# Splitting the attention row maxima on GpSimd with two maxima buffers, in a three-layer attention and expert kernel

## The chip, the cores and the metric

The kernel runs on one core of a Trainium2 chip. The metric is the device time of one execution in microseconds. A core has TensorE (PE in the profile, with PEld for its weight loads), VectorE (DVE), ScalarE (ACT), GpSimd (POOL) and SyncE (SP), which here only issues DMAs. Each engine works through its own instruction list in order, and they meet at semaphores.

## The reference, cut to what matters

The input x has 8 sequences of 512 rows of 256 numbers. Four layers follow one another; the change touches the softmax of the first, second and fourth.

```python
# layer 1: causal attention, 16 heads of 16
attn = jnp.einsum('bhqd,bhkd->bhqk', q, k) * scale
attn = jnp.where(causal, attn, -jnp.inf)
a = jnp.clip(attn, -100.0, 100.0)
m = jnp.max(a, axis=-1, keepdims=True)
e = jnp.exp(a - m)
p = e / (jnp.sum(e, axis=-1, keepdims=True) + 1e-06)
p = p + 1e-08
attn = p / jnp.sum(p, axis=-1, keepdims=True)
# layers 2 and 4: attention without a mask, then router and experts
probs = jax.nn.softmax(scores, axis=-1)
# layer 3: attention over the 8 sequences with relative positions
```

## The kernel before, in words

The function `attention` runs twice: once for layers 1 and 2 together (16 items, n = 0 to 15, one sequence of one layer each; items 0 to 7 are causal; names end in `_af`), and once for layer 4 (8 items, n = 16 to 23; names end in `_f`). Between and behind them stand the experts and layer 3, which the change leaves alone.

An item has 4 groups g of 4 heads, and a group has 4 slots kt, so 16 slots an item. All engines walk over the slots in an order written out by hand. The scores are needed twice. First as queries by keys, to get the row maximum: TensorE writes them to one of three PSUM banks `sc` (`score`, L474, with the mask at L477), and VectorE takes the negated maximum (`row_max`, L769). Slots of group g make the maxima of the group two further on, so the maxima of group g + 2 are complete when slot 3 of group g ends. Then as keys by queries, straight into the exponential: TensorE writes `sct` (`score_t`, L495), ScalarE takes the exponential (L690), VectorE clips it against a floor in causal items (`clip`, L798), and TensorE multiplies by the values (`pv`, L526). The negated maximum enters the second product as three extra rows of the stationary operand. These rows must be bf16, so the float maximum is split into three bf16 parts.

`split_max` (L771 to L786, VectorE) does this once a group, after the last `row_max` of kt = 3: a clip to plus or minus 100 in causal items (L775), a cast (L780), a subtraction (L782), a cast (L784), a subtraction (L786), each on 128x16 numbers and each waiting for the one before. One slot later TensorE transposes the parts (`use_bank` "max", L438, after `score_t` and `score` of head 0), ScalarE copies them (L655) and SP loads them into `stack_q` (L292).

GpSimd has its own list (L1176 to L1198), once an item n: `inv_std_y`, `lay_out_v`, `split` (three operations that split q or k in three parts, L1050 to L1054), `add_floor` (L1101 and L1106, causal), `inv_std_x`, `add_bias`, `scale_y`, `sum_v`, `scatter`. Three of its orders are waited for elsewhere:

- `add_floor(n - 1, 3)` completes the output of item n - 1. TensorE transposes that output at the head of slot 4 of item n (L457), waiting for `att_added` (L455).
- `inv_std_y(n - 2)` gives `shift1`, for which ScalarE waits in `norm_y` (L609, run at L616) in slots 1 and 2 of item n, in items whose predecessor but one has experts.
- ScalarE reads q or k of j = 2 and 3 from PSUM into `qkf`, which has two buffers, and waits until `split` of j - 2 has read the buffer (L664). In the opening of `attention` ScalarE reads j = 3 of item first + 1 before its first exponential (L727 to L745).

Of the kernel before, what the change touches and what calls it, by code (L numbers as in the profile page):

```python
# [49 lines left out]
def attention(nc, M, R, S, C, A, layers, first, end, units):  # L50
# [175 lines left out]
    with nc.Block(no_gpsimd_drain=True) as block:  # L226
# [533 lines left out]
        def _(dve):  # L760
            def row_max(n, g, qt, i):
                heads = score_heads(n, qt, i)
                if not heads:
                    return
                u = max_unit(n, g, qt, i)
                dve.wait_ge(S.sc_ps, u + 1)
                cols = P * (qt + 1) if causal(n) else T
                src = M.sc[u % 3][:, 0:len(heads) * cols].rearrange("p (h k) -> p h k", h=len(heads))
                nc.vector.tensor_reduce(M.neg_max[:, qt, heads[0]:heads[-1] + 1], src, AX.X, ALU.max, negate=True).then_inc(S.max_done, 1)  # L769

            def split_max(n, g):  # L771

                dve.wait_ge(S.max_done, max_unit(n, g, 3, 3) + 1)
                if causal(n):
                    nc.vector.tensor_scalar(M.neg_max[:, :, :], M.neg_max[:, :, :], -100.0, 100.0, ALU.max, ALU.min).then_inc(S.max_clip, 1)  # L775
                    dve.wait_ge(S.max_clip, NG * n + g + 1)
                if NG * n + g > 0:
                    dve.wait_ge(S.max_ps, NG * n + g)
                st = 4 * (NG * n + g)
                nc.vector.tensor_copy(M.max_parts[:, :, 0, :], M.neg_max[:, :, :]).then_inc(S.max_split, 1)  # L780
                dve.wait_ge(S.max_split, st + 1)
                nc.vector.tensor_tensor(M.max_rest[:, :, :], M.neg_max[:, :, :], M.max_parts[:, :, 0, :], ALU.subtract).then_inc(S.max_split, 1)  # L782
                dve.wait_ge(S.max_split, st + 2)
                nc.vector.tensor_copy(M.max_parts[:, :, 1, :], M.max_rest[:, :, :]).then_inc(S.max_split, 1)  # L784
                dve.wait_ge(S.max_split, st + 3)
                nc.vector.tensor_tensor(M.max_parts[:, :, 2, :], M.max_rest[:, :, :], M.max_parts[:, :, 1, :], ALU.subtract).then_inc(S.max_split, 1)  # L786

            def clip(n, g, kt, half):

# [156 lines left out]
            def slot(n, g, kt):  # L946
                s = KT * g + kt
                tn, tg = group(n, g + 2)
                pn, pg = group(n, g - 1)
                if kt > 0 and causal(n):  # L950
                    clip(n, g, kt - 1, 1)
                for i in range(4):
                    if exists(tn):
                        row_max(tn, tg, kt, i)
                    if i == 1:
                        if s - y_slot(n) in (2, 4):
                            add_y(n - 1, (s - y_slot(n) - 2) // 2)
                        if s == 9:
                            sum_key(n - 2)
                        if s == 10:  # L960
                            choose(n - 2)
                        if s == 14 and n == last:
                            place_early()
                        if 2 <= s < 6:
                            x_stats(n + 2, (s - 2,))
                    if i == 2:
                        if causal(n):
                            clip(n, g, kt, 0)
                        if kt == 2:
                            normalise(pn, pg)  # L970
                        if 4 <= s - y_slot(n) < 8:
                            y_stats(n - 1, (s - y_slot(n) - 4,))
                if kt == KT - 1 and exists(tn):
                    split_max(tn, tg)

            def split_first(j):

# [19 lines left out]
            for g in (0, 1):  # L997
                for qt in range(KT):
                    for i in range(4):
                        row_max(first, g, qt, i)  # L1000
                split_max(first, g)
            for n in range(first, end):
                if n == 1:
                    dve.wait_ge(S.consts_loaded, C.loads)
# [13 lines left out]
        def _(pool):  # L1018
# [24 lines left out]
            def split(n, j):  # L1043
                if not exists(n):
                    return
                st = 3 * (splits(n, j) - 1)
                pool.wait_ge(S.qkf_ready, 4 * n + j + 1)
                full, top = M.qkf[:, j % 2, :], M.parts[:, j, 0, :]

                nc.gpsimd.tensor_tensor(M.parts[:, j, 1, :], full, top, ALU.subtract).then_inc(S.split_step, 1)  # L1050
                pool.wait_ge(S.split_step, st + 1)
                nc.gpsimd.tensor_tensor(full, full, top, ALU.subtract).then_inc(S.split_step, 1)
                pool.wait_ge(S.split_step, st + 2)
                nc.gpsimd.tensor_tensor(M.parts[:, j, 2, :], full, M.parts[:, j, 1, :], ALU.subtract).then_inc(S.split_step, 1)  # L1054

            def lay_out_v(n, g):
                if not exists(n):
# [114 lines left out]
            for g in range(NG - 1):  # L1172
                lay_out_v(first, g)
            sum_v(first)
            split(first + 1, 0)
            for n in range(first, end):  # L1176
                if n == 1:
                    pool.wait_ge(S.consts_loaded, C.loads)
                inv_std_y(n - 2)
                lay_out_v(n, 3)  # L1180
                split(n + 1, 1)
                split(n + 1, 2)
                add_floor(n - 1, 3)
                split(n + 1, 3)
                inv_std_x(n + 2)
                add_floor(n, 0)
                add_bias(n - 1)
                scale_y(n - 2)
                lay_out_v(n + 1, 0)
                lay_out_v(n + 1, 1)  # L1190
                add_floor(n, 1)
                sum_v(n + 1)
                lay_out_v(n + 1, 2)
                add_floor(n, 2)
                if n == last:
                    inv_std_y(last - 1)
                scatter(n - 2)
                split(n + 2, 0)  # L1198
            add_bias(last)
            scale_y(last - 1)  # L1200
# [9 lines left out]
def attention_memory(nc, ctx, R, tag, dram):  # L1210

    def sb(name, shape, dt=F32):
        return ctx.enter_context(nc.sbuf_tensor(f"{name}_{tag}", shape, dt))

    def psum(name):
        return ctx.enter_context(nc.psum_tensor(f"{name}_{tag}", [P, T], F32))

    gen = [psum("gen0"), psum("gen1")]
    M = Names()
    M.q_parts_d, M.k_parts_d, M.src_d = dram  # L1220

    M.x_in = R.w1[NW - 1][:, 0, :].rearrange("p (t d) -> p t d", t=KT)
    M.xn = R.w1[NW - 1][:, 1, :].rearrange("p (t d) -> p t d", t=KT)
    M.res = sb("res", [P, KT, D])
    M.st0 = sb("st0", [P, KT, 6])
    M.mv0 = sb("mv0", [P, KT, 2])
    M.var0 = sb("var0", [P, KT])
    M.rstd0 = sb("rstd0", [P, KT])
    M.mean0, M.shift0 = sb("mean0", [P, KT]), sb("shift0", [P, KT])
    M.xnT = sb("xnT", [P, DC, T])  # L1230
    M.qkf = sb("qkf", [P, 2, T])
    M.parts = sb("parts", [P, 4, 3, T], BF16)
    M.v_st = sb("v_st", [P, KT, D])
    M.v_aug = sb("v_aug", [P, KT, H, 32])

    shared = R.w2[:, :, :, :].rearrange("p c e d -> p (c e d)")
    o1, o2 = 2 * 4 * T, 2 * 4 * T + (KT - 2) * H * 32
    M.floor = shared[:, 0:o1].rearrange("p (g h t) -> p g h t", g=2, h=4)
    M.v_later = shared[:, o1:o2].rearrange("p (t h e) -> p t h e", t=KT - 2, h=H)
    M.v_pair = shared[:, o2:o2 + 2 * D].rearrange("p (a d) -> p a d", a=2)  # L1240
    M.v_tot = shared[:, o2 + 2 * D:o2 + 3 * D]
    M.v_all = shared[:, o2 + 3 * D:o2 + 5 * D].rearrange("p (a d) -> p a d", a=2)

    M.stack_q = sb("stack_q", [99, NG, 4, T], BF16)
    M.stack_k = sb("stack_k", [99, NG, 4, T], BF16)

    M.neg_max = sb("neg_max", [P, KT, 4])
    M.max_rest = sb("max_rest", [P, KT, 4])
    M.max_parts = sb("max_parts", [P, KT, 3, 4], BF16)
    M.max_sb = sb("max_sb", [12, 2, T], BF16)  # L1250
    M.prob = sb("prob", [P, 2, 4, T])
    M.o_sb = sb("o_sb", [P, T])
    M.floor_w = sb("floor_w", [P, KT, 4])
    M.e8 = sb("e8", [P, KT, 4])
    M.den = sb("den", [P, KT, 4])
    M.rden = sb("rden", [P, KT, 4])
    M.floor_v = sb("floor_v", [P, KT, 4, HD])
    M.att = [sb(f"att{i}", [P, KT, D]) for i in range(2)]
    M.attT = sb("attT", [P, DC, T])

    M.sc = [psum("sc0"), psum("sc1"), psum("sc2")]
    M.sct = [psum("sct0"), psum("sct1")]
    M.out = psum("out")
    M.gen = gen
    M.gen_bf = [t[:, :].bitcast(BF16) for t in gen]
    return M
# [1327 lines left out]
```

## Time and profile before

| what | us |
|---|---|
| median of 3 runs (2644.34 to 2658.11) | 2650.02 |
| the profiled execution, its own time | 2654.06 |
| its span in the profile | 2652.3 |
| TensorE busy | 2465.1 (93% of the span) |
| VectorE busy | 1835.1 (69%) |
| ScalarE busy | 1438.0 (54%) |
| GpSimd busy | 1332.1 (50%) |

The two runs of `attention` fill about 40 to 1150 us and 1825 to 2370 us of the span. The profile gives each group of instructions with its line, engine and count, the waits by releaser, and a timeline of each engine. The mean granted TensorE clock was 0.971 of full speed, where 1.00 stands for 2.4 GHz and 0.50 for 1.2 GHz.

### The profile page before, as it was taken

Reading aid. Unit: us, or ns where it says so; the run is one execution under the profiler, and the core shown is the slowest. Engines: PE = TensorE matmul, PEld = TensorE weight load, DVE = VectorE, ACT = ScalarE, POOL = GpSimd, SP = SyncE. Lnnn points to the kernel's source line nnn. Section 1 sums busy time; section 2 is a strip of 40 time slices with the busy share of each in tenths; the row PEclk is TensorE's granted clock in tenths of the full one; section 3 lists DMA queues with packets and bytes.
Section 4 is the critical chain, followed back from the end, with each engine's and each line's share of the span. In section 5 each row is a group of like instructions: output and inputs, shape, how many; then the busy total and the mean of one; then the engine's idle time right before and its main releaser. Section 6 shows DMA issues by size and latency. Waiting matters only on the chain. (4 is left out here: it accounts for less than half of the span.)

```text
span 2652.3 us, 46652 instructions
## 1 busy us (share of the span) xinstructions
PE 2465.1 (93%) x15144; PEld 1430.2 (54%) x15144; DVE 1835.1 (69%) x3682; ACT 1438.0 (54%) x2991; POOL 1332.1 (50%) x1349
## 2 busy tenths in 40 slices
PE   6999999999999999989996899976999999989998
PEld 3555555554444444368886466652344444349897
DVE  5988999898788887843333457666778888844333
ACT  3666666666777777643332222113777777753332
POOL 5455666553345554246555466644235554445555
PEclk9999999999999999999998799988999999999999
DMA  5333333343434444145554000004434444335554
GB/s 161 94 109 97 109 108 101 106 117 101 121 113 126 126 130 120 53 150 193 195 177 155 22 1 17 17 24 133 120 109 131 129 129 121 94 113 168 195 195 137
DMA packets 249650, 305.92 MB, mean 115 GB/s; under 512 B 27746, under 2 KB 224577, under 8 KB 249412
## 3 DMA queue, kind: packets, MB, share of 16 engines
q1 hardware_dynamic: 237876, 275.37, 34.8%
q0 software_dynamic: 10176, 26.27, 2.8%
q8 instruction: 125, 2.05, 0.3%
q10 hardware_dynamic: 1360, 1.31, 0.2%
q14 instruction: 113, 0.93, 0.1%
HBM read 210.32 MB, written 92.84 MB: 114 GB/s over the span
## 5 line engine op out<-in xcount | busy, mean ns | idle before, releaser
L769 DVE TENSOR_REDUCE neg_max_af<-sc_af 128x1 f32<-128x512 f32 (+3 forms) x864 | 551.1, 663 | 109.5 <-PE sc_af L474 84.5
L690 ACT ACTIVATE prob_af<-sct_af 128x512 f32<-128x512 f32 (+1 forms) x864 | 484.5, 582 | 249.1 <-PE sct_af L495 137.4
L769 DVE TENSOR_REDUCE neg_max_f<-sc_f 128x1 f32<-128x512 f32 x512 | 334.0, 685 | 92.1 <-PE sc_f L474 90.1
L690 ACT ACTIVATE prob_f<-sct_f 128x512 f32<-128x512 f32 x512 | 291.0, 598 | 134.8 <-PE sct_f L495 133.0
L474 PE MATMUL sc_af<-stack_k_af,stack_q_af 96*128 96x512 bf16 (+3 forms) x1024 | 332.2, 345 | 19.3 <-DVE neg_max_af L769 13.4
L495 PE MATMUL sct_af<-stack_q_af,stack_k_af 99*128 99x512 bf16 (+3 forms) x1024 | 331.3, 346 | 5.2 <-ACT prob_af L690 4.4
L1598 PE MATMUL y_ps_e<-w_r,hT_e 128*128 x1120 | 258.5, 384 | 7.5 <-issue 5.6
L798 DVE SCALAR_TENSOR_TENSOR prob_af<-prob_af,w_r 128x512 f32<-128x512 f32 (+2 forms) x224 | 231.5, 1042 | 25.9 <-ACT prob_af L690 25.7
L526 PE MATMUL out_af<-prob_af,v_aug_af 128*32 128x512 f32 (+3 forms) x2048 | 232.3, 525 | 6.8 <-DVE prob_af L798 5.9
L1598 PEld LDWEIGHTS y_ps_e<-w_r,hT_e 128*128 128x128 f32 x1120 | 209.4, 192 | 38.4 <-issue 11.9
L495 PEld LDWEIGHTS sct_af<-stack_q_af,stack_k_af 99*128 99x128 bf16 x1024 | 100.1, 98 | 228.5 <-ACT prob_af L690 147.6
L1783 DVE TENSOR_TENSOR y_e<-y_ps_e,b_e 128x256 f32<-128x256 f32 x70 | 29.7, 425 | 279.4 <-PE y_ps_e L1598 276.7
L1611 PE MATMUL hT_ps_e<-xT_e,w_r 128*128 128x128 f32 x1856 | 219.7, 277 | 3.2 <-DMA w_r<-in_f_W_dram 2.0
L1611 PEld LDWEIGHTS hT_ps_e<-xT_e,w_r 128*128 128x128 f32 x1856 | 218.0, 194 | 7.2 <-DMA w_r<-in_f_W_dram 3.1
L474 PE MATMUL sc_f<-stack_k_f,stack_q_f 96*128 96x512 bf16 x512 | 195.4, 387 | 20.4 <-DVE neg_max_f L769 13.3
L1668 ACT ACTIVATE xT_e<-xT_ps_e 128x256 f32<-128x256 f32 x70 | 26.9, 385 | 332.4 <-PE xT_ps_e L1589 332.4
L495 PE MATMUL sct_f<-stack_q_f,stack_k_f 99*128 99x512 bf16 x512 | 195.3, 384 | 4.5 <-ACT prob_f L690 3.3
L474 PEld LDWEIGHTS sc_af<-stack_k_af,stack_q_af 96*128 96x128 bf16 x1024 | 102.1, 100 | 127.6 <-DVE neg_max_af L769 54.0
L1679 ACT ACTIVATE hT_e<-hT_ps_e,b_r 128x128 f32<-128x128 f32 x560 | 152.8, 383 | 32.1 <-issue 25.7
L1050 POOL TENSOR_TENSOR parts_af<-qkf_af,parts_af 128x512 bf16<-128x512 f32 x62 | 76.6, 1236 | 127.7 <-ACT parts_af L668 127.6
L526 PE MATMUL out_f<-prob_f,v_aug_f 128*32 128x512 f32 x1024 | 137.0, 607 | 0.8 <-ACT prob_f L690 0.7
L495 PEld LDWEIGHTS sct_f<-stack_q_f,stack_k_f 99*128 99x128 bf16 x512 | 49.6, 98 | 159.0 <-ACT prob_f L690 120.1
(373 smaller groups left out, 4744.7 us busy)
## 6 DMA issues: line engine op xcount, KB each, us to landing
w_r<-in_f_W_dram SPq DMA_DIRECT2D x66, 1024.0 KB, 5.0
stack_k_af<-k_parts_d SPq DMA_DIRECT2D x64, 384.0 KB, 4.2
k_parts_d<-parts_af SPq DMA_DIRECT2D x187, 128.0 KB
q_parts_d<-parts_af SPq DMA_DIRECT2D x96, 128.0 KB
stack_q_af<-q_parts_d SPq DMA_DIRECT2D x64, 192.0 KB, 3.0
stack_k_f<-k_parts_d SPq DMA_DIRECT2D x32, 384.0 KB, 4.3
w_next<-in_f_W_dram SPq DMA_DIRECT2D x12, 1024.0 KB, 4.9
k_parts_d<-parts_f SPq DMA_DIRECT2D x91, 128.0 KB
```

Source lines behind the costliest of these rows:

```text
L474: last = nc.tensor.matmul(bank[:, o:o + cols], M.stack_q[0:96, g, h, qt * P:qt * P + P], M.stack_k[0:96, g, h, 0:cols], start=True, stop=True)
L495: last = nc.tensor.matmul(bank[:, o:o + T - q0], M.stack_k[0:99, g, h, kt * P:kt * P + P], M.stack_q[0:99, g, h, q0:T], start=True, stop=True)
L526: last = nc.tensor.matmul(bank[32 * i:32 * i + 32, q0:T], M.v_aug[:, kt, 4 * g + i, :], M.prob[:, kt % 2, i, 0:T - q0], start=(kt == 0), s ...
L690: nc.scalar.activation(dst, src.rearrange("p (h q) -> p h q", h=len(heads)), ACT.Exp).then_inc(S.exp_done, 1)
L769: nc.vector.tensor_reduce(M.neg_max[:, qt, heads[0]:heads[-1] + 1], src, AX.X, ALU.max, negate=True).then_inc(S.max_done, 1)
L798: nc.vector.scalar_tensor_tensor(out=p, in0=p, scalar=1.0, in1=M.floor[:, g % 2, hs, kt * P:T], op0=ALU.min, op1=ALU.max).then_inc(S.clip_ ...
L1050: nc.gpsimd.tensor_tensor(M.parts[:, j, 1, :], full, top, ALU.subtract).then_inc(S.split_step, 1)
L1598: last = nc.tensor.matmul(y_ps[:, 0:D], hT[s % 2][:, c, :], w2[:, c, e, :], start=(c == 0), stop=(c == FC - 1))
L1611: last = nc.tensor.matmul(hT_ps[2 * (s % 2) + f][:, q * P:q * P + P], w1[n % NW][:, c, cols], xT[:, c, :], start=(c == 0), stop=(c == DC - 1))
L1668: nc.scalar.activation(xT[:, :, :], xT_ps[:, 0:D].rearrange("p (c t) -> p c t", c=DC), ACT.Copy).then_inc(xT_ready, 1)
L1679: last = nc.scalar.activation(hT[s % 2][:, 4 * f + q, :], hT_ps[2 * (s % 2) + f][:, q * P:q * P + P], ACT.Relu, bias=b1[:, e, 4 * f + q:4 ...
L1783: nc.vector.tensor_tensor(y[i][:, :], y_ps[:, 0:D], b2[:, e, :], ALU.add).then_inc(y_ready, 1)
```

## The change

`neg_max` gets a second buffer, chosen by g % 2. VectorE keeps the row maxima and the clip (`clip_max`, causal only), and the four operations of the split become orders of GpSimd. VectorE waits, before the first maximum of a group, until the split of the group two before is done.

```diff
                 dve.wait_ge(S.sc_ps, u + 1)
+                if qt == 0 and i == 0 and NG * n + g >= 2:
+                    dve.wait_ge(S.max_split, 4 * (NG * n + g - 1))
...
-                nc.vector.tensor_reduce(M.neg_max[:, qt, heads[0]:heads[-1] + 1], src, AX.X, ALU.max, negate=True).then_inc(S.max_done, 1)
+                nc.vector.tensor_reduce(M.neg_max[:, g % 2, qt, heads[0]:heads[-1] + 1], src, AX.X, ALU.max, negate=True).then_inc(S.max_done, 1)
...
+            def clip_max(n, g):
                 if causal(n):
+                    dve.wait_ge(S.max_done, max_unit(n, g, 3, 3) + 1)
+                    nc.vector.tensor_scalar(M.neg_max[:, g % 2, :, :], M.neg_max[:, g % 2, :, :], -100.0, 100.0, ALU.max, ALU.min).then_inc(S.max_clip, 1)
...
+            def split_max(n, g):
+
+                if not exists(n):
+                    return
+                if causal(n):
+                    pool.wait_ge(S.max_clip, NG * n + g + 1)
+                else:
+                    pool.wait_ge(S.max_done, max_unit(n, g, 3, 3) + 1)
+                if NG * n + g > 0:
+                    pool.wait_ge(S.max_ps, NG * n + g)
+                st = 4 * (NG * n + g)
+                top = M.neg_max[:, g % 2, :, :]
+                nc.gpsimd.tensor_copy(M.max_parts[:, :, 0, :], top).then_inc(S.max_split, 1)
+                pool.wait_ge(S.max_split, st + 1)
+                nc.gpsimd.tensor_tensor(M.max_rest[:, :, :], top, M.max_parts[:, :, 0, :], ALU.subtract).then_inc(S.max_split, 1)
+                pool.wait_ge(S.max_split, st + 2)
+                nc.gpsimd.tensor_copy(M.max_parts[:, :, 1, :], M.max_rest[:, :, :]).then_inc(S.max_split, 1)
+                pool.wait_ge(S.max_split, st + 3)
+                nc.gpsimd.tensor_tensor(M.max_parts[:, :, 2, :], M.max_rest[:, :, :], M.max_parts[:, :, 1, :], ALU.subtract).then_inc(S.max_split, 1)
...
             sum_v(first)
+            split_max(first, 0)
             split(first + 1, 0)
+            split_max(first, 1)
             for n in range(first, end):
...
                 lay_out_v(n, 3)
                 split(n + 1, 1)
                 split(n + 1, 2)
+                split_max(*group(n, 2))
                 add_floor(n - 1, 3)
                 split(n + 1, 3)
                 inv_std_x(n + 2)
                 add_floor(n, 0)
                 add_bias(n - 1)
                 scale_y(n - 2)
+                split_max(*group(n, 3))
                 lay_out_v(n + 1, 0)
                 lay_out_v(n + 1, 1)
                 add_floor(n, 1)
+                split_max(*group(n, 4))
                 sum_v(n + 1)
                 lay_out_v(n + 1, 2)
                 add_floor(n, 2)
...
                 scatter(n - 2)
+                split_max(*group(n, 5))
                 split(n + 2, 0)
```

GpSimd's list in a causal item, before: `split(n + 1, 2)` (3 rows) and `add_floor(n - 1, 3)` (2).

```order
L1050 TENSOR_TENSOR parts_af<-qkf_af,parts_af 128x512
L1052 TENSOR_TENSOR qkf_af<-qkf_af,parts_af 128x512
L1054 TENSOR_TENSOR parts_af<-qkf_af,parts_af 128x512
L1101 TENSOR_TENSOR floor_v_af<-floor_w_af,w_r 128x256
L1106 TENSOR_TENSOR att_af<-att_af,floor_v_af 128x4x64
```

The same place in the changed kernel:

```order
L1041 TENSOR_TENSOR parts_af<-qkf_af,parts_af 128x512
L1043 TENSOR_TENSOR qkf_af<-qkf_af,parts_af 128x512
L1045 TENSOR_TENSOR parts_af<-qkf_af,parts_af 128x512
L1059 CAST max_parts_af<-neg_max_af 128x4x4
L1061 TENSOR_TENSOR max_rest_af<-neg_max_af,max_parts_af 128x16
L1063 CAST max_parts_af<-max_rest_af 128x4x4
L1065 TENSOR_TENSOR max_parts_af<-max_rest_af,max_parts_af 128x4x4
L1112 TENSOR_TENSOR floor_v_af<-floor_w_af,w_r 128x256
L1117 TENSOR_TENSOR att_af<-att_af,floor_v_af 128x4x64
```

The split of the maxima of group 2 stands between the two. In the same way one stands ahead of `split(n + 2, 0)` at the item's end.

GpSimd's list in the first opening, before: `split(first + 1, 0)`, `lay_out_v(first, 3)`, and the first row of `split(first + 1, 1)`.

```order
L1050 TENSOR_TENSOR parts_af<-qkf_af,parts_af 128x512
L1052 TENSOR_TENSOR qkf_af<-qkf_af,parts_af 128x512
L1054 TENSOR_TENSOR parts_af<-qkf_af,parts_af 128x512
L1067 TENSOR_TENSOR v_aug_af<-v_st_af,ones 128x4x4x16
L1074 TENSOR_TENSOR w_r<-v_aug_af 128x128
L1076 TENSOR_TENSOR w_r<-w_r,v_aug_af 128x128
L1050 TENSOR_TENSOR parts_af<-qkf_af,parts_af 128x512
```

The same place in the changed kernel:

```order
L1041 TENSOR_TENSOR parts_af<-qkf_af,parts_af 128x512
L1043 TENSOR_TENSOR qkf_af<-qkf_af,parts_af 128x512
L1045 TENSOR_TENSOR parts_af<-qkf_af,parts_af 128x512
L1059 CAST max_parts_af<-neg_max_af 128x4x4
L1061 TENSOR_TENSOR max_rest_af<-neg_max_af,max_parts_af 128x16
L1063 CAST max_parts_af<-max_rest_af 128x4x4
L1065 TENSOR_TENSOR max_parts_af<-max_rest_af,max_parts_af 128x4x4
L1078 TENSOR_TENSOR v_aug_af<-v_st_af,ones 128x4x4x16
L1085 TENSOR_TENSOR w_r<-v_aug_af 128x128
L1087 TENSOR_TENSOR w_r<-w_r,v_aug_af 128x128
L1041 TENSOR_TENSOR parts_af<-qkf_af,parts_af 128x512
```

The last row, the head of `split(first + 1, 1)`, now follows the split of the maxima of group 1 of item first. The split of group 0's maxima stands ahead of the first row.

## Rows read from the trace of the kernel before

**Rows 1.** One window: busy PE, PEld, DVE, ACT, POOL (us), PEclk, DMA share, GB/s

```profile
300.00:400.00 100.00, 97.57 (x865) 54.20 (x864) 91.12 (x173) 67.31 (x125) 57.60 (x53) 1.00 0.37 106
```

**Rows 2.** Waits of TensorE in the causal items, layer 2, layer 4: us, times, longest

```profile
PE out_af L526 <- DVE prob_af L798: 5.9, 12, 0.7
PE sc_af L474 <- DVE neg_max_af L769: 4.8, 9, 1.0
...
PE sc_af L474 <- DVE neg_max_af L769: 8.0, 7, 1.5
...
PE sc_f L474 <- DVE neg_max_f L769: 12.8, 11, 2.6
```

**Rows 3.** Groups by line: two operations; busy us, mean ns | idle before

```profile
L1154 POOL TENSOR_TENSOR own_r<-rank_r,onehot_r 128x16 f32<-128x16 f32 x12 | 2.7, 222 | 11.9 <-ACT rank_r L645 11.9
...
L798 DVE SCALAR_TENSOR_TENSOR prob_af<-prob_af,w_r 128x512 f32<-128x512 f32 (+2 forms) x224 | 231.5, 1042 | 25.9 <-ACT prob_af L690 25.7
```

**Rows 4.** Timeline of VectorE, where row maxima are complete: start us, us, instruction

```profile
287.23 0.17 DVE L775 TENSOR_SCALAR neg_max_af<-neg_max_af 128x16 f32<-128x16 f32 x1
...
339.54 0.41 DVE L775 TENSOR_SCALAR neg_max_af<-neg_max_af 128x16 f32<-128x16 f32 x1
...
358.70 0.17 DVE L775 TENSOR_SCALAR neg_max_af<-neg_max_af 128x16 f32<-128x16 f32 x1
```

**Rows 5.** Timeline of GpSimd in causal items

```profile
283.28 1.07 POOL L1101 TENSOR_TENSOR floor_v_af<-floor_w_af,w_r 128x256 f32<-128x256 f32 x1
284.43 0.72 POOL L1106 TENSOR_TENSOR att_af<-att_af,floor_v_af 128x256 f32<-128x256 f32 x1
...
337.05 1.16 POOL L1050 TENSOR_TENSOR parts_af<-qkf_af,parts_af 128x512 bf16<-128x512 f32 x1
...
353.64 1.15 POOL L1054 TENSOR_TENSOR parts_af<-qkf_af,parts_af 128x512 bf16<-128x512 f32 x1
```

**Rows 6.** Timeline of TensorE: the transposes at the head of slot 4

```profile
288.00 1.06 PE L457 MATMUL gen_af<-ident,att_af 128*128 128x128 f32 x4
...
358.40 0.61 PE L457 MATMUL gen_af<-ident,att_af 128*128 128x128 f32 x4
```

**Rows 7.** Two windows around the idle time of slots 2 and 3 (columns of Rows 1)

```profile
282.00:284.00 2.00, 1.00 (x9) 0.28 (x11) 2.00 (x5) 0.92 (x2) 1.92 (x3) 1.00 0.55 190
286.00:288.00 2.00, 2.00 (x11) 1.11 (x10) 1.86 (x6) 0.62 (x3) 0.00 (x0) 0.50 0.03 9
```

**Rows 8.** Timelines of the two openings: GpSimd, ScalarE, VectorE, TensorE

```profile
48.59 0.72 POOL L1067 TENSOR_TENSOR v_aug_af<-v_st_af,ones 128x256 f32<-128x256 f32 x1
...
50.35 1.15 POOL L1050 TENSOR_TENSOR parts_af<-qkf_af,parts_af 128x512 bf16<-128x512 f32 x1
...
52.81 1.15 POOL L1054 TENSOR_TENSOR parts_af<-qkf_af,parts_af 128x512 bf16<-128x512 f32 x1
...
57.38 0.69 ACT L668 ACTIVATE qkf_af<-gen_af,no_bias 128x512 f32<-128x512 f32 x1 [1.77 <-PE gen_af L413]
...
60.17 0.28 DVE L775 TENSOR_SCALAR neg_max_af<-neg_max_af 128x16 f32<-128x16 f32 x1
...
1834.98 0.39 PE L474 MATMUL sc_f<-stack_k_f,stack_q_f 96*128 96x512 bf16 x1 [2.64 <-DVE neg_max_f L769]
...
1844.93 0.60 ACT L690 ACTIVATE prob_f<-sct_f 128x512 f32<-128x512 f32 x1 [0.34 <-PE sct_f L495]
...
1846.05 0.26 DVE L780 CAST max_parts_f<-neg_max_f 128x16 bf16<-128x16 f32 x1
```

**Rows 9.** Timelines of GpSimd, VectorE and ScalarE where an item of layer 2 begins

```profile
961.11 0.25 POOL L1022 TENSOR_SCALAR mean_r<-mv_r 128x4 f32<-128x4 f32 x1 [1.99 <-DVE mv_r L862]
...
961.55 0.17 DVE L780 CAST max_parts_af<-neg_max_af 128x16 bf16<-128x16 f32 x1
...
962.86 0.20 POOL L1027 TENSOR_TENSOR shift_r<-mean_r,rstd_r 128x4 f32<-128x4 f32 x1
...
968.09 1.09 ACT L616 ACTIVATE x_out_r<-tmp_r,shift_r,rstd_r 128x256 f32<-128x256 f32 x2
```

More of the change, by code:

```diff
@@ L766, in row_max @@
                 dve.wait_ge(S.sc_ps, u + 1)
+                if qt == 0 and i == 0 and NG * n + g >= 2:
+                    dve.wait_ge(S.max_split, 4 * (NG * n + g - 1))
                 cols = P * (qt + 1) if causal(n) else T
                 src = M.sc[u % 3][:, 0:len(heads) * cols].rearrange("p (h k) -> p h k", h=len(heads))
-                nc.vector.tensor_reduce(M.neg_max[:, qt, heads[0]:heads[-1] + 1], src, AX.X, ALU.max, negate=True).then_inc(S.max_done, 1)
-            def split_max(n, g):
-                dve.wait_ge(S.max_done, max_unit(n, g, 3, 3) + 1)
+                nc.vector.tensor_reduce(M.neg_max[:, g % 2, qt, heads[0]:heads[-1] + 1], src, AX.X, ALU.max, negate=True).then_inc(S.max_done, 1)
+            def clip_max(n, g):
                 if causal(n):
[L775 to L786, printed above, removed]
+                    dve.wait_ge(S.max_done, max_unit(n, g, 3, 3) + 1)
+                    nc.vector.tensor_scalar(M.neg_max[:, g % 2, :, :], M.neg_max[:, g % 2, :, :], -100.0, 100.0, ALU.max, ALU.min).then_inc(S.max_clip, 1)
             def clip(n, g, kt, half):
@@ L973, in slot @@
                 if kt == KT - 1 and exists(tn):
-                    split_max(tn, tg)
+                    clip_max(tn, tg)
             def split_first(j):
@@ L1000, in _ @@
                         row_max(first, g, qt, i)
-                split_max(first, g)
+                clip_max(first, g)
             for n in range(first, end):
@@ L1245, in attention_memory @@
     M.stack_k = sb("stack_k", [99, NG, 4, T], BF16)
-    M.neg_max = sb("neg_max", [P, KT, 4])
+    M.neg_max = sb("neg_max", [P, 2, KT, 4])
     M.max_rest = sb("max_rest", [P, KT, 4])
```

## The prediction, made before the changed kernel was run

> **What bounds the kernel now.** I began with the busy times in a window of 100 us inside the causal items [rows 1]. TensorE is busy for 97.57 of 100 us there, VectorE for 91.12, ScalarE for 67, GpSimd for 58. So TensorE sets the time of `attention`, and any engine can cost time only by making TensorE stand. The reader should see how little can be won: 2.4 us in 100.
>
> Next I read what TensorE waits for [rows 2]. For the row maxima it waits 4.8 us in the causal items, 8.0 in layer 2 and 12.8 in layer 4, and for VectorE's clip of the probabilities 5.9. Together these are 31.5 us, and that is all that a faster VectorE could give back directly. Then I went along the timelines of VectorE, GpSimd and TensorE at each place where the changed order puts a split of maxima, because GpSimd's list runs in order and everything behind the new wait moves.
>
> **What leaves VectorE.** 96 groups lose four operations each, and in the causal timeline each takes 0.17 us with a start every 0.21 us, so 0.83 us a group (estimated from the four starts behind the clip at 287.23 [rows 4]). The work is on VectorE, hidden behind TensorE except where it has a wait in [rows 2]. Most of these waits stand elsewhere than behind a split: in layers 2 and 4 the recurring ones are in the slot in which the router's choice runs. The causal ones come as pairs of 0.5 us in slots 2 and 3, when VectorE has had no idle time since the slot 15 before, so 0.83 us less backlog should remove a part. Bounds: nothing, and 4.8 + 5.9 = 10.7 us. I take 4 us, nearer to nothing than to all, because TensorE waits there for two different operations of VectorE and GpSimd's long operations stretch VectorE's there too.
>
> **What comes on GpSimd.** The nearest row is a two-input operation on 128x16 numbers, 0.22 us [rows 3]; with 0.08 us between dependent ones four take 1.2 us. By itself this is hidden, as GpSimd has 42 us in 100 free [rows 1]. What is not hidden is the wait ahead of it. There are three places.
>
> **1. The output of the item before, at slot 4.** `add_floor(n - 1, 3)` now stands behind `split_max(n, 2)`, which needs the maxima that are complete only as slot 3 ends. Before, the floor was added by 284.43 + 0.72 = 285.15 [rows 5], and TensorE used it at 288.00 [rows 6]: 2.9 us of cover. Now the clip ends at 287.40 [rows 4], the split takes 1.2, `add_floor` takes 1.07 + 0.08 + 0.72 = 1.9 [rows 5], so it ends at 290.5. TensorE stands at the transposes from 288.00 on, with all of slot 4 queued behind them: 2.5 us. In the next item TensorE comes at 358.40, while the clip ends at 358.87: 358.87 + 1.2 + 1.9 = 362.0, so 3.6 us. The first form is that of the items with a low clock just before slot 4, five of the eight (n = 1, 2, 3, 6, 7), the second that of n = 4, 5 and 8. Sum: 5 x 2.5 + 3 x 3.6 = 23.3 us. VectorE comes up to 0.83 us earlier, since it has no split in its way; TensorE comes earlier as well where its own waits went. I take 0.5 us off each of the eight: **19 us**. Bounds: 8 x 1.5 = 12 and 8 x 3.6 = 29.
>
> Could GpSimd be late for this? `split(n + 2, 0)` began at 337.05 [rows 5] and must now wait for the clip that ends at 339.95 [rows 4] and the split, so until 341.2, 4.1 us later. The list behind it ended at 353.64 + 1.15 = 354.8, and `lay_out_v` had 1 us of idle time that takes up some, so it ends by 358.9 at the latest. That is level with the clip's 358.87. It adds nothing, or up to half a microsecond.
>
> The Trainium skill, page "SBUF — State Buffer", section "SBUF: two separate sides", says that VectorE and GpSimd share a port pair as an exclusive lock for whole instructions, which a VectorE operation takes if it has two SBUF inputs or runs in a two-port mode. The traces bear it out (the same clip of the maxima took 0.41 us and 0.17 us [rows 4], the longer one while GpSimd was in a split [rows 5]). By this rule one clip of probabilities, 1.04 us on average [rows 3], could stand before the second operation of `add_floor` each time, and the eight stalls would grow by 8 us. My sum goes without, because VectorE's clips of slot 4 need exponentials whose scores TensorE computes only at the head of the slot, so the first is about as late as the addition's end.
>
> **2. The two openings.** ScalarE must read j = 3 of item first + 1 before its first exponential, and waits for `split(first + 1, 1)`. That order now stands behind the split of group 1's maxima. In the first opening ScalarE read at 57.38, and group 1's maxima were complete at 60.17 [rows 8]. VectorE and TensorE will be earlier, as the split of group 0 leaves VectorE; it held TensorE for 2.64 us in the second opening [rows 8], and in the first, which has other gaps, I take 1.6. So: maxima at 58.5, clip and split to 60.0, `lay_out_v(first, 3)` 1.8 (48.59 to 50.35) to 61.8, `split` 3.6 (50.35 to 53.96) to 65.4, against 57.38: ScalarE is 8 us late and TensorE, with two banks for ScalarE, almost as much. I take 7. In the second opening TensorE's wait of 2.64 us [rows 8] goes and the maxima of group 1 are there at 1843 in place of 1846.05; then 1.2 + 0.7 (the first operation of `lay_out_v` alone) + 3.6 + 1.4 (two reads of 0.69) gives the first exponential at 1850 against 1844.93. The split that began at 1846.05 and held VectorE for about another 1.7 us goes too, so I take 3. Together **10 us**; bounds 4 and 14.
>
> **3. The head of an item in layers 2 and 4.** `inv_std_y` stands behind `split_max` and `split(n + 2, 0)`. The latter ran in idle time before 961.11; now it follows the maxima, complete at 961.5 [rows 9]: 961.5 + 1.2 + 3.6 = 966.3, and the chain from 961.11 to 963.06 (2.0 us) ends at 968.3 or 968.4. ScalarE wants it at 968.09. That is 0.3 us, 12 times, so **3 us**; bounds 0 and 10 (0.8 us if the small operations take twice as long).
>
> Other orders that move have more cover: `split_max(n, 3)` stands behind `scale_y`, but TensorE wants it only in slot 9; `sum_v` and `lay_out_v(n + 1, 2)` are used a slot or more later, and SP's stores of parts and its loads of the stacks, which follow the splits by up to 6 us, are needed at slot 8. VectorE's new wait asks for a split that ended two slots before. If SP's cover were gone, a load of maxima rows would be late, which is in the range.
>
> **The clock.** Where TensorE idles for 1.0 of 2 us, the granted clock falls to 0.50 (1.2 GHz) 3 us later [rows 7]. Two microseconds at half the clock cost 1 us, as TensorE is busy for all of it. Five of the eight items have such a stretch. A stall of 2.5 us should bring it in all eight: 3 x 1.0, **3 us**, bounds -5 and 10.
>
> **Sum.** 19 + 10 + 3 + 3 - 4 = 31 us on the profiled execution's own time of 2654.06, so 2685. That execution lies 4 us over the median of 2650.02, so against the median I forecast **2681 us**, 1.2% slower.
>
> **The rivals.** What measures here can tell from no change is about 0.5%, 13 us.
>
> A: *VectorE's relief is worth more than the stalls.* If TensorE had its 31.5 us of waits from the backlog that the splits leave, and with them the low clocks of five items (5 us), up to 36 us could go, and if half of it does and `add_floor` is covered, the kernel gains 18 us: 2632. It decides if TensorE's arrival at slot 4 is later than the end of `add_floor`; against it stands that the clip ends at most 0.6 us before TensorE comes, with 3.1 us of work behind it. Chance 0.06.
>
> B: *The stalls are made good later.* In a stall VectorE and ScalarE catch up, so the pairs of 0.5 us and the idle time of the router's slot might vanish, and the openings gain what they lose. Then 12 + 4 + 0 - 10 = 6 us: 2656. Chance 0.14.
>
> C: *GpSimd is late in the causal items by the lock.* Each of its operations may wait for a clip, and the queue is level already. With 1.5 us more a stall, 3 us more in the openings, 0.8 us at each head and the clock: 31 + 12 + 3 + 7 + 3 = 56: 2706. Chance 0.15.
>
> The forecast itself has 0.65.
>
> **How the numbers follow.** All low bounds of the forecast together are 12 + 4 + 0 - 5 - 10.7, about zero, all high ones over 60; neither is likely. Eight in ten lie between 2656, where B's centre is, and 2702, just short of C. Slower by over 0.5% (above 2663) takes the forecast but for a small low end, C, and a piece of B: 0.82. Within 0.5%: most of B and the rest, 0.13. Faster: 0.05.
>
> **What would show it.** Right: in the changed profile TensorE waits at L457's successor for GpSimd's `att_added`, eight times, 2 to 3.6 us each, in the first 650 us; ScalarE's read of j = 3 starts near 65 us, and the first exponential of layer 4 some 5 us later than before; the four GpSimd operations take 0.2 to 0.4 us each; TensorE's waits for maxima shrink from 25.6 us, those of the router's slot stay. Wrong: no wait at the slot 4 transposes, or the split's end there later than 2 us behind the maxima, or a new wait of TensorE for `max_parts` or for `stack_q`.

## The result and the profile after

The changed kernel takes **2690.34 us** (median, 2681.15 to 2694.1) against 2651.19 us for the kernel before on the same chip: 1.43% slower, ratio 1.0143 with a 95% interval of [1.0111, 1.0175]. The forecast was 2681 us, 1.2% slower. The profiled execution of the changed kernel took 2681.15 us (span 2679.0), against 2654.06 (2652.3) before. A ratio and its interval are taken from the runs of normal speed alone (three stray ones of 2993.59, 3130.29 and 7398.88 us in the groups below are left out), and the ratio is not the quotient of the two medians.

Busy times (the page's first part), changed kernel:

```profile
PE 2466.2 (92%) x15144; PEld 1431.4 (53%) x15144; DVE 1748.0 (65%) x3298; ACT 1440.0 (54%) x2991; POOL 1406.2 (52%) x1733
```

The change did what it says: 384 instructions left VectorE for GpSimd. Its price is in what TensorE waits for (whole span: us, times, longest):

```profile
PE gen_af L457 <- POOL att_af L1117: 24.3, 8, 3.0
...
PE sct_f L495 <- ACT prob_f L690: 10.5, 8, 7.4
...
PE sct_af L509 <- ACT w_r L697: 9.4, 1, 9.4
```

None of the three stands like this in the kernel before. The first is slot 4 of items 1 to 8, where the outputs of the eight causal items (0 to 7) are transposed. Here is one, from GpSimd's, VectorE's and TensorE's timelines (start us, us, instruction, in brackets the idle time before it and its releaser), where before stood [rows 4 to 6]:

```profile
442.65 1.15 POOL L1045 TENSOR_TENSOR parts_af<-qkf_af,parts_af 128x512 bf16<-128x512 f32 x1
...
444.99 0.17 DVE L777 TENSOR_SCALAR neg_max_af<-neg_max_af 128x16 f32<-128x16 f32 x1
...
445.23 0.20 POOL L1059 CAST max_parts_af<-neg_max_af 128x16 bf16<-128x16 f32 x1 [1.42 <-DVE neg_max_af L777]
445.51 0.22 POOL L1061 TENSOR_TENSOR max_rest_af<-neg_max_af,max_parts_af 128x16 f32<-128x16 f32 x1
445.80 0.20 POOL L1063 CAST max_parts_af<-max_rest_af 128x16 bf16<-128x16 f32 x1
446.07 0.22 POOL L1065 TENSOR_TENSOR max_parts_af<-max_rest_af,max_parts_af 128x16 bf16<-128x16 f32 x1
446.25 0.62 POOL L1112 TENSOR_TENSOR floor_v_af<-floor_w_af,w_r 128x256 f32<-128x256 f32 x1
446.95 0.72 POOL L1117 TENSOR_TENSOR att_af<-att_af,floor_v_af 128x256 f32<-128x256 f32 x1
...
447.82 1.09 PE L457 MATMUL gen_af<-ident,att_af 128*128 128x128 f32 x4 [3.04 <-POOL att_af L1117]
```

GpSimd is free at 443.80 and could add the floor at once, as experiment 1 lets it. It stands 1.42 us for the clip that ends at 445.16, then splits for 1.1 us, then adds. TensorE came at 444.78.

Behind this stall TensorE runs at its lower clock (columns as in [rows 1]; PEclk is the third number from the end, 0.50 is 1.2 GHz). After the same 3.04 us in the item two earlier, which ended at 301.39, there is no such stretch:

```profile
449.00:451.00 2.00, 2.00 (x28) 1.28 (x30) 0.89 (x1) 1.52 (x3) 0.27 (x1) 0.50 0.82 198
451.00:453.00 2.00, 2.00 (x20) 1.24 (x13) 0.33 (x1) 1.11 (x3) 1.92 (x2) 0.50 0.09 24
453.00:455.00 2.00, 2.00 (x15) 1.32 (x14) 1.84 (x2) 1.10 (x3) 1.92 (x2) 0.84 0.00 0
...
303.00:305.00 2.00, 2.00 (x33) 1.42 (x22) 1.19 (x1) 2.00 (x5) 1.41 (x1) 1.00 0.72 180
```

The first opening, ScalarE's read of j = 3 and TensorE behind it [rows 8], and TensorE's first long wait in the second:

```profile
59.93 0.22 POOL L1065 TENSOR_TENSOR max_parts_af<-max_rest_af,max_parts_af 128x16 bf16<-128x16 f32 x1
...
61.86 1.15 POOL L1041 TENSOR_TENSOR parts_af<-qkf_af,parts_af 128x512 bf16<-128x512 f32 x1
...
65.56 0.69 ACT L668 ACTIVATE qkf_af<-gen_af,no_bias 128x512 f32<-128x512 f32 x1 [10.74 <-POOL parts_af L1045]
...
67.47 1.18 PE L509 MATMUL sct_af<-stack_q_af,stack_k_af 3*128 3x512 bf16 x2 [9.40 <-ACT w_r L697]
...
1869.71 0.61 PE L495 MATMUL sct_f<-stack_q_f,stack_k_f 99*128 99x512 bf16 x1 [7.43 <-ACT prob_f L690]
```

Where the time went, by the start of the same instruction in the two profiles. The transposes at slot 4 of item 1: 145.46 before, 155.04 after, so +9.6, of which 3.04 is the first stall and 6.5 the opening (1.1 of these lie ahead of the first scores, at 36.97 and 38.07, where the two kernels do the same). The last transposes of causal and layer 2 attention: 1151.15 and 1184.53, +33.4, so what follows slot 4 of item 1 gave 23.8 more, 23.1 of it by slot 4 of item 9 (708.60 and 741.31). Layer 4 is read from two groups of TensorE, the first operation of the layer (L404) and the transposes of slot 4 (L457), before and after (xcount: min/median/max ns, first to last start in us):

```profile
L404 PE MATMUL gen_f<-ident,w_next x64: 270/273/447, 1794.6 to 2224.0; 128*128 128x128 f32 x64
L457 PE MATMUL gen_f<-ident,att_f x64: 270/272/327, 1922.2 to 2365.5; 128*128 128x128 f32 x64
```

```profile
L404 PE MATMUL gen_f<-ident,w_next x64: 270/273/421, 1814.7 to 2247.6; 128*128 128x128 f32 x64
L457 PE MATMUL gen_f<-ident,att_f x64: 270/272/327, 1945.7 to 2389.7; 128*128 128x128 f32 x64
```

570.9 before, 575.0 after: +4.1. The touched parts so cost 33.4 + 4.1 = 37.5 us, close to the 39 between the medians. In the two profiles the difference is only 27, since the experts and layer 3, which the change doesn't touch, took 13 us less in this one execution (from 1794.6 - 1151.2 = 643.4 to 1814.7 - 1184.5 = 630.2).

### The profile page after: what moved, and what is told of

It reads as the page before. It is cut to its first block and busy times, and to the rows that moved or that the text cites. A ratio compares the mean times of both kernels' runs of the same rounds, so it can differ in the third digit from the quotient of the medians.

```text
span 2679.0 us, 46746 instructions
## 1 busy us (share of the span) xinstructions
PE 2466.2 (92%) x15144; PEld 1431.4 (53%) x15144; DVE 1748.0 (65%) x3298; ACT 1440.0 (54%) x2991; POOL 1406.2 (52%) x1733
## 5 line engine op out<-in xcount | busy, mean ns | idle before, releaser
L1059 POOL CAST max_parts_af<-neg_max_af 128x16 bf16<-128x16 f32 x64 | 12.7, 198 | 303.0 <-DVE neg_max_af L771 203.8
```

The source lines that it names most:

```text
L1059: nc.gpsimd.tensor_copy(M.max_parts[:, :, 0, :], top).then_inc(S.max_split, 1)
```

## The experiments

Each ran against the kernel before on the same chip, whose medians were 2649.27 (experiments 1 to 4), 2648.7 (5 and 6) and 2648.78 us (7 and 8). The changed kernel was not run again beside them; the kernel before stood at 2651.19 beside it, so a difference from its 2690.34 may be off by some 2 us. The order in a list is read from the medians, and where the time lies from one profiled execution of each kernel. Theory Q: the cost is in the place of GpSimd's wait in its list. Rival W: the cost is the work that GpSimd now does. "An item takes" means from slot 4 of one item to slot 4 of the next.

### 1. The floor ahead of the split, at slot 4

```diff
-                split_max(*group(n, 2))
                 add_floor(n - 1, 3)
+                split_max(*group(n, 2))
```

> The changed kernel with one edit: in GpSimd's list add_floor(n - 1, 3) stands ahead of split_max(n, 2) again. Theory Q (the cost is what is queued behind a split's wait): TensorE's eight waits of 3.0 us at the transposes of slot 4 vanish, and with them the low clock that follows five of them (0.50 for up to 7 us, 1.5 to 2.8 us an item); 24 + 9 = 33 us less than the changed kernel's 2690, so about 2657 to 2663; the opening's waits of 9.4 and 7.4 us stay. Rival W (the cost is the split's work on GpSimd, through the shared port or its slower operations): the order alone changes little, within 8 us of 2690.

Measured: 2653.96 us, ratio 1.0020 [1.0001, 1.0039]; 36 us of the loss are gone, by two lines that change places, 3 us more than the range expected. TensorE's waits there, and the windows behind one:

```profile
PE gen_af L457 <- POOL att_af L1117: 7.0, 7, 1.0
```

```profile
435.00:437.00 2.00, 2.00 (x33) 1.42 (x22) 1.19 (x2) 2.00 (x5) 1.43 (x1) 1.00 0.65 159
437.00:439.00 2.00, 2.00 (x22) 1.11 (x23) 2.00 (x3) 1.72 (x5) 1.92 (x2) 1.00 0.74 212
```

Seven stalls shrink from 3.04 to 1.0 us and the eighth is gone: 24.3 - 7.0 = 17.3 us. No item has a low clock behind slot 4 any more. From slot 4's transposes to the next ones of the same item takes 13.76 us in seven items; with the change it took 13.76, 15.31, 13.76, 15.38, 16.48, 16.48 and 16.46, and 17.16 against 14.40 in the eighth: 14.1 us, in six items and not in the five of my expectation, which had 9 us for it. 17.3 + 14.1 = 31.4 us, and the last transposes of this attention move by 31.2 (1184.53 to 1153.37). So nearly half of what this edit gives back in attention is the clock.

### 2. The split of group 1 behind split(first + 1, 1), at the openings

```diff
-            split_max(first, 1)
             for n in range(first, end):
...
                 split(n + 1, 1)
+                if n == first:
+                    split_max(first, 1)
                 split(n + 1, 2)
```

> The changed kernel with one edit: the split of the maxima of group 1 of the first item of each run of attention stands behind split(first + 1, 1). Theory Q: ScalarE's read of j = 3 no longer waits 10.7 us, TensorE's waits of 9.4 and 7.4 us vanish, 6.5 + 3.5 = 10 us less than the changed kernel, about 2680; the eight stalls of 3.0 us stay. Rival W: no change from 2690 (within 3 us), since the work is the same.

Measured: 2668.81 us, ratio 1.0072 [1.0047, 1.0097], 21.5 us less than the change, twice what was expected. Slot 4 of item 1 comes at 146.88 in place of 155.04 (8.2 us), and layer 4 takes 564.1 us from its first operation to its last transposes in place of 575.0 (10.9). The eight stalls are untouched:

```profile
PE gen_af L457 <- POOL att_af L1117: 24.2, 8, 3.0
```

The miss is in the second opening. I had priced it by the kernel before, but the edit not only takes away the stall of 7.43 us. Behind that stall TensorE worked at half the clock from 1869.7 to 1877, which costs 3.6 us, and with the edit it doesn't. One window of the changed kernel, then the same part of layer 4 with the edit:

```profile
1873.00:1875.00 2.00, 2.00 (x10) 0.24 (x10) 0.87 (x2) 1.07 (x2) 0.00 (x0) 0.50 0.00 0
```

```profile
1863.00:1865.00 2.00, 1.88 (x13) 0.41 (x5) 1.71 (x4) 1.06 (x3) 0.00 (x0) 1.00 0.50 154
```

7.4 + 3.6 = 11.0 us against the 10.9 measured. Layer 4 is then 6.8 us faster than before, so the +4.1 between the two kernels was a loss of 10.9 less a gain of 6.8. Experiment 7 shows where the gain comes from.

### 3. Both edits

> Both edits at once. Theory Q: the costs add, 33 + 10 us less than the changed kernel, and what is left against the kernel before is VectorE's relief: 7 causal items by 0.5 to 1 us and about 5 us in the two openings, so 2640 to 2650, up to 0.4% faster than before. Rival W: still 2675 or more. If the relief is worth much more than I think (rival A of the prediction), 2632 or less.

Measured: 2637.74 us, ratio 0.9949 [0.9931, 0.9968]: faster than both kernels, and 2 us under the range expected. The two costs are separate and nearly add up: 36.4 + 21.5 = 57.9 us below the change by the parts, 52.6 measured.

### 4. The waits without the work

VectorE splits as before, with one buffer; GpSimd only waits, at the six places where the change has a split.

```diff
+            def wait_max(n, g):
+
+                if exists(n):
+                    pool.wait_ge(S.max_split, 4 * (NG * n + g + 1))
```

> The kernel before (the split of the maxima stays on VectorE) with waits alone added to GpSimd's list, at the six places where the changed kernel has its splits. No work moves. Theory Q: the wait is the cost, so TensorE stalls about 2.9 us at the eight transposes and 7 to 10 us in the openings, and VectorE's relief is missing: 2690 to 2697. Rival W: nothing but the work costs, so 2651 within 8 us.

Measured: 2688.33 us, ratio 1.0148 [1.0123, 1.0174], the change's own time to 2 us. TensorE's waits and one slot 4:

```profile
PE gen_af L457 <- POOL att_af L1111: 23.0, 8, 2.9
```

```profile
379.00 1.09 PE L457 MATMUL gen_af<-ident,att_af 128*128 128x128 f32 x4 [2.87 <-POOL att_af L1111]
```

So the loss is there without any work moved: the place of the wait in the list makes it. It doesn't say that the four operations are free. In the changed kernel 1.1 of the 3.04 us are the split on GpSimd; here the wait is for VectorE's split, 0.8 us, which takes its place in the chain ahead of the floor. But the run says more. An item takes 75.1 us here, with 2.87 of stall and 2.85 of low clock behind it (16.61 - 13.76): without them 69.4. With the change it is 72.40 - 3.04 = 69.4 as well, and before it was 70.33 in an item with no low clock. So the microsecond an item that I had put down to VectorE's relief is there although VectorE keeps all its work.

### 5. The floor one place further up

On top of both edits:

```diff
+                add_floor(n - 1, 3)
                 split(n + 1, 2)
-                add_floor(n - 1, 3)
                 split_max(*group(n, 2))
```

> Both edits, and add_floor(n - 1, 3) moved further up, ahead of split(n + 1, 2) instead of behind it. In the version with both edits TensorE still waits 1.0 us for it at slot 4 of the eight causal items, because the three rows of split(n + 1, 2), 3.8 us, stand ahead of it. Theory (only the place in GpSimd's list makes the wait): floor_w of that item is there at 419.8, so the addition ends near 421.7 against TensorE's 424.6, the wait is 0, the item's period 69.3 to 69.4 us instead of 70.35, and the median falls from 2638 to about 2630 (2627 to 2633). Rival (the split of q and k that is now 1.9 us later is what TensorE or SP's stores need next): the 1.0 us goes and another wait of 1 to 2 us comes at slots 5 to 8, the median stays at 2636 to 2645.

Measured: 2625.46 us, ratio 0.9918 [0.9895, 0.9940], the best version, and 1.5 us under the range expected. TensorE no longer waits at slot 4; an item takes 69.71 us.

```profile
420.63 0.60 PE L457 MATMUL gen_af<-ident,att_af 128*128 128x128 f32 x4
```

Of the 1.0 us an item 0.65 are kept (70.36 to 69.71); TensorE's next wait, for the clip of the probabilities in slot 4, is now 0.7 us long. The seven items from slot 4 of item 1 to slot 4 of item 8 make 5 us of the 12 between the medians, and slot 4 of item 1 comes 2.4 us earlier (141.81 against 144.23); the rest lies in no one place that I found.

### 6. Both edits, the split on VectorE

Experiment 4 with its waits at the places of experiment 3.

> As the version with both edits, GpSimd's waits and order included, but the four operations of the split stay on VectorE with one buffer. What it is slower by than that version (2638) is what the relief of VectorE alone is worth. Theory: the causal items lose their relief of 1.0 us each (8 us) and the few microseconds at the opening of layer 4, so 2646 to 2652. Rival R (the relief is worth nothing in itself, the gain over the kernel before came from the changed order of GpSimd's list): 2636 to 2641. Rival W (a longer stay on VectorE makes the wait at slot 4 longer and brings the low clock behind it back): over 2658.

Measured: 2634.16 us, ratio 0.9954 [0.9936, 0.9972], against 0.9949 for the same order with the split on GpSimd: no difference that these runs can tell. Rival R holds: GpSimd's waits, added to the kernel before with nothing else changed, make it 0.5% faster, and moving the work adds nothing to that. This was against my theory. What was open now was which of the waits does it.

### 7. One wait at an item's end, and the waits of the openings alone

First the kernel before with GpSimd's wait for group 5's split ahead of split(n + 2, 0) only:

> The kernel before with one thing added: GpSimd waits for the split of group 5 of the item before (VectorE's, as ever) before split(n + 2, 0). Theory C (what the version with waits alone gained came from GpSimd's long operations no longer meeting VectorE's clip and split at an item's end): the subtraction of the maxima there takes 0.18 us again, not 1.02, the pairs of 0.5 us waits in slots 2 and 3 go, the eight items run at 70.4 us in place of 71.1 although 1.0 us is waited at slot 4, so 5 to 7 us off the before of the same chip: about 2643. Rival (the gain is in the waits at the openings and in mid-item): within 3 us of before, or slower by up to 8 us from the eight stalls.

Then the kernel before with the two waits of each opening only:

> The kernel before with the waits of the two openings alone, at the places that the version with both edits uses. Theory C: split(first + 1, 0) no longer meets VectorE's split of group 0's maxima, whose first cast was stretched at the opening of layer 4, and the wait of 2.6 us of TensorE behind it goes; 2 us less at the first opening and 6 at the second: about 2641. Rival (the openings gained from where the later splits lie, not from these waits, or the gain is not there): within 3 us of before, 2649.

Measured: 2641.59 us, ratio 0.9961 [0.9938, 0.9983], and 2639.41 us, ratio 0.9975 [0.9956, 0.9994]. Both are as theory C has them. VectorE at an item's end, in the kernel before (where GpSimd's split(n + 2, 0) runs since 337.05 [rows 5], its third row from 340.00), then with the wait, with the first row of that split:

```profile
340.20 1.02 DVE L782 TENSOR_TENSOR max_rest_af<-neg_max_af,max_parts_af 128x16 f32<-128x16 f32 x1
...
340.00 1.18 POOL L1054 TENSOR_TENSOR parts_af<-qkf_af,parts_af 128x512 bf16<-128x512 f32 x1
```

```profile
336.93 0.18 DVE L782 TENSOR_TENSOR max_rest_af<-neg_max_af,max_parts_af 128x16 f32<-128x16 f32 x1
...
337.60 1.16 POOL L1050 TENSOR_TENSOR parts_af<-qkf_af,parts_af 128x512 bf16<-128x512 f32 x1 [3.54 <-DVE max_parts_af L786]
```

The subtraction of 1.02 us (clip 0.41 [rows 4]) is stretched while a long operation of GpSimd runs, 0.18 without one. An item gains 0.95 us (71.10 to 70.15 on average over seven) though TensorE now waits 1.0 us at slot 4. Part of it is the clock: before, five of the seven took 71.3 to 71.8 us, each with a stretch at 0.50 like that of [rows 7]; now the clock stays at 1.00 in all of them, which is 0.8 us an item. At the opening of layer 4 it is the casts of group 0, before with GpSimd's rows beside them, then with the waits:

```profile
1831.19 1.16 POOL L1052 TENSOR_TENSOR qkf_f<-qkf_f,parts_f 128x512 f32<-128x512 f32 x1
1831.35 1.03 DVE L780 CAST max_parts_f<-neg_max_f 128x16 bf16<-128x16 f32 x1
1832.41 0.17 DVE L782 TENSOR_TENSOR max_rest_f<-neg_max_f,max_parts_f 128x16 f32<-128x16 f32 x1
1832.43 1.18 POOL L1054 TENSOR_TENSOR parts_f<-qkf_f,parts_f 128x512 bf16<-128x512 f32 x1
1832.62 1.01 DVE L784 CAST max_parts_f<-max_rest_f 128x16 bf16<-128x16 f32 x1
1833.67 0.65 DVE L786 TENSOR_TENSOR max_parts_f<-max_rest_f,max_parts_f 128x16 bf16<-128x16 f32 x1
```

```profile
1812.99 0.17 DVE L780 CAST max_parts_f<-neg_max_f 128x16 bf16<-128x16 f32 x1
1813.20 0.17 DVE L782 TENSOR_TENSOR max_rest_f<-neg_max_f,max_parts_f 128x16 f32<-128x16 f32 x1
1813.41 0.17 DVE L784 CAST max_parts_f<-max_rest_f 128x16 bf16<-128x16 f32 x1
```

These four took 3.0 us in place of 0.8, and held back the maxima of group 1; that was TensorE's wait of 2.64 us [rows 8]. A second wait for maxima, of 1.75 us at 1848.43, stands in the same way behind the split that began at 1846.05. Behind each of the two the clock was low before, and with the waits it stays at 1.00 there:

```profile
1837.00:1839.00 2.00, 2.00 (x4) 0.98 (x4) 2.00 (x4) 0.00 (x0) 0.86 (x1) 0.55 0.39 130
...
1849.00:1851.00 2.00, 2.00 (x8) 0.54 (x7) 1.77 (x3) 0.86 (x2) 0.00 (x0) 0.51 0.00 0
```

Layer 4 takes 564.4 us with the waits (1777.5 to 2341.9). It took 570.9 before, 1 us of the difference being ahead of the first scores, and 570.4 with the one wait at an item's end, which leaves this opening alone. Slot 4 of item 1 comes at 143.53 in place of 145.46; there TensorE's wait for the parts of the maxima (L438) falls from 2.3 to 0.2 us.

### 8. The fastest order, the split on VectorE

Experiment 5's order with waits in place of splits.

> Split of the maxima on VectorE, all six waits of GpSimd, and add_floor(n - 1, 3) ahead of split(n + 1, 2). The counterpart of the fastest version (2625, split on GpSimd). Theory C (moving the four operations is worth nothing, only the places are): 2620 to 2628. Rival R (once TensorE doesn't wait at slot 4, VectorE's 0.83 us a group count): 2630 to 2636.

Measured: 2639.2 us, ratio 0.9972 [0.9952, 0.9993], against 0.9918 [0.9895, 0.9940] with the split on GpSimd. Here rival R of this run holds, though the time lies 3 us above its range: the same move that was worth nothing in experiment 6 is worth 14 us by the medians. An item takes 70.69 us against 69.71. In the profiles the seven items up to slot 4 of item 8 make 8.8 us, with one low clock of 1.6 us, the opening ahead of them 3.1 and layer 4 3.1; of these two I can't say that they come from the move (1.5 us of layer 4's stand ahead of its first scores). In slot 4 TensorE waits for the clip of the probabilities, first here, then in experiment 5:

```profile
293.16 1.06 PE L526 MATMUL out_af<-prob_af,v_aug_af 128*32 128x512 f32 x8 [1.64 <-DVE prob_af L798]
```

```profile
287.18 1.06 PE L526 MATMUL out_af<-prob_af,v_aug_af 128*32 128x512 f32 x8 [0.71 <-DVE prob_af L789]
```

0.9 us more, which is the 0.83 us of the four operations, just ahead of that clip on VectorE. In experiments 3 and 6, with 1.0 us of wait at slot 4, VectorE has that time anyway: slot 4 of item 7 comes at 566.37 and 566.38.

## Why the prediction was right, and where its steps were off

**The stalls at slot 4** (19 us, bounds 12 to 29): 24.3, all eight of 3.0 us. The mechanism and the place were right. The two forms of 2.5 and 3.6 did not come about: in each item TensorE now waits for GpSimd, and all have the same order of events. add_floor took 1.42 us in place of the 1.9 taken from [rows 5]. TensorE came at 444.78, 0.38 us ahead of the clip's end at 445.16, where my first form, that of five items, had it 0.6 us behind that end; so the stalls came out longer in spite of the quicker floor.

The rule of the port pair (the Trainium skill, page "SBUF — State Buffer", section "SBUF: two separate sides") would have put a clip of VectorE ahead of the floor's second operation and added 8 us. The row at 446.95 has 0.72 us directly behind the first: no clip came between, and leaving it out was right. Where I did not look for the same rule was in the gain: experiment 7's rows, 1.02 and 0.18 us for one subtraction with two SBUF inputs, with and without a long operation of GpSimd beside it, agree with it.

**The openings** (10 us): 6.5 + 4.1 = 10.6. ScalarE read j = 3 at 65.56, forecast 65.4; the first exponential of layer 4 came 54.4 us after the layer's first operation in place of 50.3, 4 us later, forecast 5. The 4.1 is what two larger terms leave: by experiment 2 the wait costs 10.9 in layer 4, the 3.6 of the clock included, for which the forecast had nothing here, and 6.8 come back.

**The head of an item in layers 2 and 4** (3 us, bounds 0 and 10): 0.7. An item of layer 2 takes 65.43 us in both profiles (708.60 to 774.03, 741.31 to 806.74), and from slot 4 of item 9 to the last transposes it is 442.55 before and 443.22 after. The chain did move by as much as forecast, to where it just suffices (in [rows 9] the same two rows are 5 us apart):

```profile
1000.80 0.20 POOL L1018 TENSOR_TENSOR shift_r<-mean_r,rstd_r 128x4 f32<-128x4 f32 x1
...
1001.04 1.10 ACT L616 ACTIVATE x_out_r<-tmp_r,shift_r,rstd_r 128x256 f32<-128x256 f32 x2
```

**The clock** (3 us, bounds -5 and 10): 8.7, the term most off. 14.1 us behind the stalls, less the 5.4 us that the items before lost in theirs (71.3 to 71.8 us an item against 70.33). I took one price, 1.0 us, for each; measured were 0, 1.6 and 2.7 us.

**VectorE's relief** (-4 us): size near by luck, cause wrong. Items 2 to 8 gained 0.97 us each, about 7 us. But experiments 4 and 6 have this gain with VectorE's work unchanged. It came from the new waits, which keep split(n + 2, 0) off the end of the item, where before it stretched VectorE's small operations. The step that failed is "0.83 us less backlog should remove a part": at that point of the changed kernel TensorE waited for GpSimd and gave VectorE the time. The row of 0.41 us [rows 4] beside GpSimd's of 337.05 [rows 5] had shown the collision; I used it only for a possible cost.

Sum: 24.3 + 10.6 + 0.7 + 8.7 - 6.8 = 37.5, as by the starts, against 31. That it came so close is in part luck: the clock cost 5.7 us more than forecast, and 2.8 of them came back in a gain whose cause I had wrong. TensorE's waits for row maxima shrank as forecast, to 8.8 + 8.8 = 17.6 us in the whole span. Rival A had the relief alone in mind and its point of decision, TensorE later than the floor, never came. Rival B fell: the stalls at slot 4 were not made good later (+0.7 us behind them), and of the openings only the 6.8 us in layer 4, which have their own cause. Rival C's mechanism was absent: in the item shown nothing held GpSimd between the clip's end and the floor's, and all eight stalls are alike.

## What to carry to other kernels

In an in-order queue the place of a wait is what costs: four operations of 0.2 us moved at no cost that these runs can tell (experiments 3 and 6), but one wait put ahead of an addition that TensorE needs next cost 36 us. When work is moved to another engine's list, put it behind everything that is ready and wanted earlier; here three such moves of lines turned 1.4% slower into 0.8% faster. And to credit a gain to moved work, run the new waits with the work left where it was: here they alone made the kernel 0.5% faster, and moving the work began to pay only when TensorE no longer waited for something else in the same slot.

## What was not expected of the hardware

Equal stalls of TensorE are not followed by equal clocks: after 3.04 us of idle time it ran at full clock in two items, lost 1.6 us in two and 2.7 us in four; after 2.87 us (experiment 4) it lost 2.8 to 2.9 us in seven of eight; after one wait of 1.0 us (experiments 1 and 3) nothing, though in the kernel before 1.0 us of idle time in a 2 us window was followed by 0.50 [rows 7]. What the stalls of 3.04 us differ in was not settled. And a wait on GpSimd can make a kernel faster, by moving its long operations off the short ones of VectorE: one 128x16 subtraction took 1.02 us or 0.18, one cast 1.03 or 0.17.
